# One burst of value products for four units of keys, with seven probability buffers, four of them in the expert weights' memory

## The reference, cut to what matters

```python
x = x + 0.5 * ffn(layernorm(x))      # layer 1: router picks 1 of 8 experts per token
x = x + attention(layernorm(x))      # 16 heads of 8, rotary positions, causal softmax
x = x + 0.5 * ffn(layernorm(x))      # layer 2: the same weights again
# attention, per head
score = einsum('bqd,bkd->bqk', q, k)
score = where(causal, score, -inf)
attn = softmax(score / sqrt(8)); out = einsum('bqk,bkd->bqd', attn, v); out @ Wo.T
# ffn, per token
h = relu(xn @ W1[e] + b1[e]); y = (h @ W2[e] + b2[e]) * gate
```

## Time and profile before

| | us |
|---|---|
| median of 3 runs (range) | 932.06 (926.17 to 937.27) |
| the profiled execution, its own time | 934.51 |
| its span, from first to last instruction | 932.7 |
| PE, DVE, ACT, POOL busy in the span | 770.6, 633.5, 556.0, 352.5 |

### The profile page before, as it was taken

The page is one execution under the profiler, slowest core; times in us unless marked ns, Lnnn a source line. Parts: engine busy times, 40 slices in busy tenths (PEclk is TensorE's granted clock), DMA queues, the critical chain, the costliest instruction groups (busy, mean ns, idle before and its releaser), DMA issues. The chain is left out here.

```text
span 932.7 us, 16893 instructions
## 1 busy us (share of the span) xinstructions
PE 770.6 (83%) x5318; PEld 416.8 (45%) x5318; DVE 633.5 (68%) x1750; ACT 556.0 (60%) x1196; POOL 352.5 (38%) x635
## 2 busy tenths in 40 slices
PE   9578884287289999999999999999999989488784
PEld 7477774144013333333333333333333329477774
DVE  4645663599587887788787787778778306656663
ACT  2078883144126667676667766776767563178883
POOL 5077762078411332233222332233223310177762
PEclk9589998599559999999999999999999779589997
DMA  9821220325740210222022211221020000521120
GB/s 313 179 53 50 50 45 8 91 78 141 196 99 2 52 41 13 53 52 53 7 48 53 53 23 31 53 53 37 17 53 2 2 16 18 97 52 51 49 45 8
DMA packets 41267, 54.51 MB, mean 58 GB/s; under 512 B 8019, under 2 KB 33757, under 8 KB 39776
## 3 DMA queue, kind: packets, MB, share of 16 engines
q1 hardware_dynamic: 33680, 42.99, 19.4%
q0 software_dynamic: 4992, 9.44, 4.2%
q10 hardware_dynamic: 2512, 1.06, 0.5%
HBM read 36.19 MB, written 17.79 MB: 58 GB/s over the span
## 5 line engine op out<-in xcount | busy, mean ns | idle before, releaser
L1341 DVE CUSTOM_DVE_ANT_0 cst<-psS,cst 128x768 bf16<-128x768 f32 (+7 forms) x512 | 364.2, 755 | 103.3 <-PE psS L1215 100.6
L1305 ACT ACTIVATE prob<-psST 128x512 f32<-128x512 f32 (+3 forms) x768 | 323.8, 496 | 141.8 <-PE psST L1240 138.6
L1254 PE MATMUL a_psO<-prob,vs 128*32 128x512 f32 (+3 forms) x1536 | 167.6, 509 | 0.9 <-POOL prob L1426 0.7
L1425 POOL TENSOR_TENSOR a_gate<-a_zeros 1x1 f32<-1x1 f32 x128 | 23.4, 183 | 334.4 <-ACT prob L1305 334.4
L1240 PE MATMUL psST<-a_qs,ks 75*128 75x512 bf16 (+1 forms) x480 | 124.0, 327 | 5.6 <-ACT prob L1305 3.3
L1215 PE MATMUL psS<-ks,a_qs 72*128 72x512 bf16 (+2 forms) x480 | 116.5, 332 | 5.3 <-DVE a_rowmax L1341 5.2
L761 POOL DMA_INDIRECT f_row<-rows,f_there_number x78 | 77.6, 996 | 102.3 <-DMA rows<-tok 79.2
L1215 PE MATMUL psS<-ks,qs 72*128 72x512 bf16 (+3 forms) x288 | 76.6, 360 | 24.4 <-DMA qs<-q_split 17.1
L647 PE MATMUL f_ps_wide<-f_xnT,f_w1s 128*128 128x128 f32 x624 | 86.6, 284 | 2.2 <-ACT f_xnT L711 2.2
L1240 PE MATMUL psST<-qs,ks 75*128 75x512 bf16 (+3 forms) x288 | 79.6, 349 | 6.5 <-ACT prob L1305 5.4
L647 PEld LDWEIGHTS f_ps_wide<-f_xnT,f_w1s 128*128 128x128 f32 x624 | 79.5, 200 | 3.3 <-ACT f_xnT L711 3.3
(11 more groups left out here) (154 smaller groups left out, 983.6 us busy)
## 6 DMA issues: line engine op xcount, KB each, us to landing
ks<-k_split SPq DMA_DIRECT2D x48, 192.0 KB
a_qs<-q_split SPq DMA_DIRECT2D x60, 96.0 KB
k_split<-p_part SPq DMA_DIRECT2D x40, 128.0 KB, 2.3
rows<-tok SPq DMA_DIRECT2D x8, 524.0 KB, 9.3
qs<-q_split SPq DMA_DIRECT2D x36, 96.0 KB
q_split<-p_part SPq DMA_DIRECT2D x24, 128.0 KB, 2.3
w<-in_Wb SPq DMA_DIRECT2D x1, 2064.0 KB, 7.5
w<-in_W SPq DMA_DIRECT2D x1, 2048.0 KB, 12.6
```

The costliest lines, as they stand in the source:

```text
L1254: last = nc.tensor.matmul(psO[32 * h:32 * h + 32, c0:c0 + w], vs[r][:, j, h, :], prob[:, u % RING, h, 0:w], start=(j == 0), stop=(u + 1 in ...
L1305: nc.scalar.activation(prob[:, u % RING, h, 0:w], psST[(u * QH + h) % 3][:, 0:w], ACT.Exp, scale=SCALE).then_inc(exp_done, 1)
L1341: last = nc.vector.tensor_tensor_reduce(out=out[:, a * CH:a * CH + width], in0=ps[:, a * CH:a * CH + width], in1=mask_row[:, S - width:], ...
```

## The change

`plan` puts weighs only after head 0 of units 1, 5 and 9, and then four of them in a row: units 8 to 11 of the stage before, units 0 to 3, and units 4 to 7. `att` is raised for all four before `spread()` is called. `prob` becomes a ring of `PRING` = 7 buffers over all units of all stages; the four new ones lie in `n.w1` and `n.w2`. `exps` waits until unit u - 7 has been weighed. The copy out of `psO` and one `turn_out` come one unit later. Because the weights are overwritten, layer 2 loads W1, W2 and b2 again (`load_experts`), issued by SP after the table and before the wait for `rows_ready`; DVE and ACT wait for them before the first tile.

```diff
+PRING, GROUP = 7, 4
-LOADS = 5
+EXPERT_LOADS, LOADS = 3, 5
@@ ffn, DVE and ACT
-            if r == 0:
-                dve.wait_ge(n.weights_loaded, 16 * LOADS)
+            dve.wait_ge(n.weights_loaded, 16 * (LOADS + r * EXPERT_LOADS))
@@ ffn, SP
             if r == 0:
                 load_weights(sp, n)
+            else:
+                load_experts(sp, n)
@@ attend
+        lent = [w[:, :, :].rearrange("p e w -> p (e w)")[:, i * QH * CH:(i + 1) * QH * CH]
+                .rearrange("p (h c) -> p h c", h=QH) for w in (n.w1, n.w2) for i in range(2)]
+        n.prob_ring = ([n.prob[:, i, :, :] for i in range(RING)] + lent)[:PRING]
@@ plan
-                if h == 0:
-                    if u >= LAG:
-                        found.append(("weigh", u - LAG, 0))
-                        att += WEIGH_COST * units[u - LAG][3]
-                    elif not first:
-                        found.append(("weigh", u - LAG, 1))
-                        att += WEIGH_COST * units[u - LAG + UN][3]
+                if h == 0 and u % GROUP == LAG - 1:
+                    for v in range(u - LAG - GROUP + 1, u - LAG + 1):
+                        if v >= 0:
+                            found.append(("weigh", v, 0))
+                            att += WEIGH_COST * units[v][3]
+                        elif not first:
+                            found.append(("weigh", v, 1))
+                            att += WEIGH_COST * units[v + UN][3]
                 spread()
@@ EXTRAS
-    ... (5, "turn_out", 0, True) ...
+    ... (6, "turn_out", 0, True) ...
@@ tensor engine, after the last stage
-        weigh(NST - 1, (NST - 1) % RING, UN - 2)
-        weigh(NST - 1, (NST - 1) % RING, UN - 1)
+        for u in range(UN - GROUP, UN):
+            weigh(NST - 1, (NST - 1) % RING, u)
@@ exps
-            wait(act, pv_done, s * UN + u - 2)
+            wait(act, pv_done, s * UN + u - PRING + 1)
@@ ACT's stage
-                if u == 1 and not first:
+                if u == LAG and not first:
                     copy_out(s - 1, 1)
-                if u == half_end[0] + 1:
+                if u == half_end[0] + LAG:
                     copy_out(s, 0)
```

More of the change, by code:

```diff
@@ L223, in load_weights, with load_experts @@
         sp.wait_ge(n.x_loaded[b], 16)
+    load_experts(sp, n)
+    for there, source in ((n.cst[:, HEAD_W:], n.const[:, HEAD_W:]), (n.wproj[:, :, :], n.Wp)):
+        sp.dma_start(there, source).then_inc(n.weights_loaded, 16)
+def load_experts(sp, n):
     for there, source in ((n.w1[:, :, :], n.Wb1), (n.w2[:, :, 0:FB * D], n.W2),
-                          (n.w2[:, :, FB * D:], n.b2.partition_broadcast(P)),
-                          (n.cst[:, HEAD_W:], n.const[:, HEAD_W:]), (n.wproj[:, :, :], n.Wp)):
+                          (n.w2[:, :, FB * D:], n.b2.partition_broadcast(P))):
         sp.dma_start(there, source).then_inc(n.weights_loaded, 16)
@@ L695, in _ @@
             act.wait_ge(experts_known, 1)
-            if r == 0:
-                act.wait_ge(n.weights_loaded, 16 * LOADS)
+            act.wait_ge(n.weights_loaded, 16 * (LOADS + r * EXPERT_LOADS))
             def normalise(t, k):
@@ L1111, in attention @@
     AHEAD = tile_total * tile_cost[0]
-    EXTRAS = [(1, "turn_max", 1, True), (4, "turn_out", 1, False), (5, "turn_out", 0, True),
+    EXTRAS = [(1, "turn_max", 1, True), (4, "turn_out", 1, False), (6, "turn_out", 0, True),
               (7, "turn_max", 0, False)]
@@ L1141, in attention, with prob @@
     MP = KINDS * QH * CB
-    prob, psST, psS = n.prob, n.psST, n.psS
+    psST, psS = n.psST, n.psS
+    def prob(s, u):
+        return n.prob_ring[(s * UN + u) % PRING]
     rowmax = sb("rowmax", [P, QH, TB])
@@ L1254, in weigh @@
                 last = nc.tensor.matmul(psO[32 * h:32 * h + 32, c0:c0 + w], vs[r][:, j, h, :],
-                                        prob[:, u % RING, h, 0:w], start=(j == 0),
+                                        prob(s, u)[:, h, 0:w], start=(j == 0),
                                         stop=(u + 1 in half_end))
@@ L1301, in exps @@
             ch, j, q0, w = units[u]
-            wait(act, pv_done, s * UN + u - 2)
+            wait(act, pv_done, s * UN + u - PRING + 1)
             for h in range(QH):
                 act.wait_ge(scored, s * SC + u * QH + h + 1)
-                nc.scalar.activation(prob[:, u % RING, h, 0:w], psST[(u * QH + h) % 3][:, 0:w], ACT.Exp,
+                nc.scalar.activation(prob(s, u)[:, h, 0:w], psST[(u * QH + h) % 3][:, 0:w], ACT.Exp,
                                      scale=SCALE).then_inc(exp_done, 1)
@@ L1422, in mask @@
             pool.wait_ge(exp_done, s * SC + (u + 1) * QH)
-            part = prob[:, u % RING, :, 0:P]
+            part = prob(s, u)[:, :, 0:P]
             nc.gpsimd.tensor_tensor(gate[:, u:u + 1], zeros[0:1, 0, 0:1], zeros[0:1, 0, 1:2], ALU.add)
```

## The result

The changed kernel takes 1170.64 us (median of 4 runs, 1168.96 to 1174.75) against 934.66 for the kernel before beside it: a ratio of 1.254, with a 95% interval of 1.244 to 1.265. The forecast was slower, 1085, with a range of 980 to 1155. The direction was right and the size was not: the time lies outside the range, on the side of the third rival (the clock falls after every burst, 1150).

A forecast was written before the change was run, and what follows sets the result against it. PE was taken as the bound, DVE second. The profiled 934.5 us plus 81 for the queue's order, 7 for first and last stages and 65 for the clock gave 1087.5, or 1085 against the median; range 980 to 1155.

The forecast's parts named there:

- the third rival: Middle stages: clock falls after every burst or stays low over a stretch, 130 us instead of 65: 1150; chance 0.17.
- PE is the bound, and boundaries are worth something: Attention's middle: PE bounds, DVE second; each weigh boundary removed saves 0.19 us, 1.7 us a stage.
- The ring, the masks and the reload cost nothing: Seven buffers, masks two units ahead and layer 2's weight reload: no cost; an uncovered reload up to 20 us once.
- The queue's order adds 5.8 us to a stage: Middle stages: bursts and tiles in PE's in-order queue make engines wait, 36.1 us against 30.3; +81 over 14 stages.
- The clock: "I take one and a half" falls of 3.1 us a stage, +65: Middle stages: thin PE work between bursts drops the clock, 1.5 falls a stage of 3.1 us each, +65 over 14.
- the stretch of 65% (after W0 to W3): Between the second and third bursts: PE work of 7.1 us in 11.0; not among the two expected to lose the clock.
- the two of 55 and 59%: After the first and third bursts: PE work 4.7 us in 8.5 and 4.8 in 8.1; clock expected to fall there.
- the 36.1 of the schedule: One middle stage by the queue's order, without clock falls: 10.9 + 13.4 + 11.8 us, boundary savings included.
- the 75 to 85% expected: Sign to look for: PE's busy share in the middle down from 95% to 75 or 85%.
- First and last stage, +7: First stage's two bursts +4 us; last stage, no tiles but three bursts that starve ACT, +3.
- the 1087.5 of the sum: Whole kernel: profiled 934.5 + 81 + 7 + 65 us; against the median, 1085.
- The rival that the clock holds (1020): Middle stages: queue order as worked out, no clock falls: 932 + 81 + 7 = 1020; chance 0.29.

The follow-up runs named there:

- bursts of two: Changed kernel with two weighs a burst and five buffers: 1055.0 us, ratio 1.126; with tiles spread evenly as well, 985.6 us, ratio 1.049.
- two runs with fillers: Changed kernel with an added unused 128-row matmul ahead of every score, 1099.6 us, or ahead of every second score, 1093.6 us.
- the run with all fillers: Changed kernel with an added unused matmul on all 128 rows ahead of every score: 1099.6 us, ratio 1.173 to the kernel before.
- the kernel before with doubled scores: Kernel before the change, with every score matmul issued twice into the same PSUM buffer: 1027.9 us in one run, against 930.8.

## Why the prediction was right and wrong

- **PE is the bound, and boundaries are worth something.** Right. 0.19 was taken for a boundary, 0.23 measured with bursts of two. PE is still the engine that the others wait for, but no longer because it always has work: in the order of the change it waits too.
- **The ring, the masks and the reload cost nothing.** Right: ratio 1.004 (0.998 to 1.009) for these parts alone. Layer 2 was even 3.2 us shorter in the profiled run of the changed kernel; the cause is open.
- **The queue's order adds 5.8 us to a stage.** Borne out, as far as the rows reach. The times behind a burst came to within 0.1 us as long as the clock held, and two runs with fillers lead to 35.5 us against 36.1, by extrapolation. The terms hold small errors: the sum for a burst gives 2.5 and 3.8 us where 2.4 and 3.7 were written, and in the run with all fillers, at full clock, the first kind took 2.3 (545.50 to 547.79). The DMA of the maxima was 2.2 us instead of 1.9.
- **The clock: "I take one and a half" falls of 3.1 us a stage, +65.** This is the step that failed. The mechanism was right and its count was not. The clock fell after each of the three bursts, in the stretch of 65% (after W0 to W3) as in the two of 55 and 59%, and 60% of the middle was at 1.2 GHz. The stage became 46.5 us by the stretches above (46.1 in the regular ones), not 36.1 + 4.65: 10 us for three falls, 3.3 each. With the slow first of them, the 14 middle stages cost 224.9 us more than before and not 81 + 65 = 146: 79 are missing here. The 10 us rest on the 36.1 of the schedule; by the extrapolated 35.5 they would be 10.6. The price of one fall was nearly right, but by luck, since it was made up otherwise. I had 1 us for the rest of the stretch and 2.2 for the burst. In the stage shown the three bursts are 0.8, 0.7 and 2.0 us longer, 3.5 together, and 6.5 lie in the stretches, since once the clock is down PE, at half speed, is the bound there as well. That is also why PE's busy share fell only to 88% and not to the 75 to 85% expected.
- **First and last stage, +7.** 9.5 and 6.1, 15.6 together. Of the 9.5, 3.5 lie ahead of the first stage, in code that the change leaves alone (SP's very first load of maxima starts at 264.01 instead of 260.51). From its second load to the first for stage 1 it takes 23.3 us instead of 17.3, at a clock of 0.57 instead of 0.92: here the lower clock, which I had not counted, shows. In the last the mean clock is 0.79 where it was 0.80, and what made it 6.1 longer instead of 3 stays open.
- Together: 79 in the middle stages, 8.6 at the two ends and ahead of them, less 3.2 in layer 2, are the 84 us between the 1087.5 of the sum and the profiled run's 1171.7.

The rival that the clock holds (1020) had 0.29; the one with three falls (1150) only 0.17. What spoke for the latter was in the trace: the last stage of the kernel before lost its clock with PE busy 80%, and I had all three stretches thinner than that, yet let the busiest of them count as safe. The range ended 5 us above that rival, with no room for its own error.

By the Trainium skill, TensorE: Matmul & The Clock Gate, table on why this matters, idle gaps of PE between bursts of matmuls lose the clock. The idle times of PE in the stage shown are all under a microsecond, and the clock fell three times a stage: the measurement decides against this row as the whole rule. By the Trainium skill, TensorEngine Tiling (Array Packing), Key Properties, a change of tiling mode drains the array; the 0.23 us saved for each boundary removed, a switch out and a switch in, agrees.

## What to carry to other kernels

Before grouping instructions to save a switch, follow one period of every in-order queue that they stand in, with the prices of the trace: what was saved per boundary here was 0.23 us, and with that gain in it the new order still made a stage 5 to 6 us longer at full clock. If PE becomes less busy between the groups, put in the clock as a price of its own, with a fall behind every group as one of the cases (here three in a stage, 10 us), and let the range reach beyond that case. Where an engine's busy time grows while its instruction count stays, read the granted clock first.

## What was not expected of the hardware

- The same number of added matmuls, with the same columns in the same places, gave 1218.4 and 1236.7 us with the granted clock at 0.74 to 0.80 (from 500 us on) when they used 75 rows of the array, and 1099.6 with 0.97 when they used 128. The profile's busy share of PE was 92% in the first and 90% in the second, and in 34.36 us of the first stage of the kernel before with doubled scores PE was busy for 34.33, at a clock of 0.50. So the busy share of the profile does not tell whether the clock holds. The fillers differ from the repeated scores in their operands too (constants, and weights of their own), so that the rows alone are the cause is not shown.
- Useless matmuls made two kernels faster: 1170.6 to 1099.6, and 1080.8 to 1020.8.
- Within a burst, a pass of the float32 weigh follows the one before in 0.44 us for 512 columns: 24 records (six passes, three units) took 2.80 us, the last 0.6 of which is one matmul's own length (605 ns), and the other five passes 0.44 each.
- The same instructions in the same order took 33.0 or 41.8 us a stage within one run, by the clock alone.
